# Scores of the next attention layer between the chunks of the MoE before it, on one Trainium2 core

## The reference, cut to what matters

```
h = layernorm(x) ; h = h @ ternary(w1).T + b1 ; h = gelu(h) ; h = layernorm(h) ; out = h @ ternary(w2).T + b2
```

## Time and profile before

| | us |
|---|---|
| median of 3 runs | 1383.3 (1379.87 to 1383.82) |
| the profiled execution | 1383.42 |
| its span, first to last instruction | 1381.6 |
| PE busy | 1198.1 (87%) |
| DVE busy | 927.3 (67%) |
| ACT busy | 697.0 (50%) |
| POOL busy | 269.1 (19%) |
| mean granted PE clock | 0.948 of full |

### The profile page before, as it was taken

One profiled execution on the slowest core, in us unless ns is written; L12 is line 12 of the kernel. 1 busy time (PEld: TensorE's weight loads), 2 busy tenths in 40 slices (PEclk: granted clock), 3 DMA queues, 4 the chain that ended last, 5 costly groups with the idle time before them and its releaser, 6 DMA issues.

```text
span 1381.6 us, 26337 instructions
## 1 busy us (share of the span) xinstructions
PE 1198.1 (87%) x7977; PEld 634.2 (46%) x8062; DVE 927.3 (67%) x2470; ACT 697.0 (50%) x1268; POOL 269.1 (19%) x560
## 2 busy tenths in 40 slices
PE   3436999999889998899999999999999979989876
PEld 1222223323356655445554555556666534445445
DVE  5867678687465555767778777755555476668676
ACT  2221676776644434556656666663222226666543
POOL 2332211211000012222332332110000211222112
PEclk7565999999999999999999999999999989999988
DMA  8312222310000003313333322100000202221001
GB/s 208 123 51 73 101 59 99 121 35 20 1 1 1 0 1 120 105 53 105 121 94 109 96 77 71 49 3 4 1 1 0 76 12 67 78 77 44 3 0 31
DMA packets 65199, 79.14 MB, mean 57 GB/s; under 512 B 5483, under 2 KB 58068, under 8 KB 64602
## 3 DMA queue, kind: packets, MB, share of 16 engines
q1 hardware_dynamic: 65098, 77.89, 18.0%
HBM read 45.27 MB, written 31.72 MB: 56 GB/s over the span
## 4 chain that ended last, share of the span: by engine, by line
PE 60%; issue 14%; DVE 8%; DMA 6%; ACT 5%; DVEq 3%; POOL 2%; SPq 1%; POOLq 1%; another core or an unknown queue 0%; ACTq 0%
PE bank L1633 11%; PE bank L1618 10%; PE bank L1602 9%; PE bank L1785 6%; PE bank L1786 6%; PE bank L1803 5%; PE bank L1586 3%; DMA KS<-scr_k 3%; PE bank L1620 2%; PE bank L1522 1%; ACT PT L921 1%; DVE M L1198 1%; PE bank L1582 1%; DVE N L1035 1%; PE bank L1516 1%
## 5 line engine op out<-in xcount | busy, mean ns | idle before, releaser
L921 ACT ACTIVATE PT<-bank 128x512 f32<-128x512 f32 (+1 forms) x784 | 425.3, 568 | 257.3 <-PE bank L1620 186.9
L1602 PE MATMUL bank<-KS,QS 125*128 125x512 bf16 (+3 forms) x1024 | 311.2, 332 | 37.1 <-DVE M L1195 13.6
L1198 DVE TENSOR_REDUCE M<-bank 128x1 f32<-128x512 f32 (+2 forms) x400 | 257.5, 684 | 89.3 <-PE bank L1602 53.1
L1195 DVE CUSTOM_DVE_ANT_0 masked_scores<-bank,maskw 128x384 bf16<-128x384 f32 (+1 forms) x384 | 228.6, 622 | 93.7 <-PE bank L1602 85.2
L1618 PE MATMUL bank<-QS,KS 128*128 128x256 bf16 (+1 forms) x953 | 277.4, 320 | 12.3 <-ACT PT L921 8.4
L1633 PE MATMUL bank<-PT,VA 128*32 128x512 f32 (+3 forms) x2048 | 211.6, 485 | 1.3 <-ACT PT L921 1.0
L1618 PEld LDWEIGHTS bank<-QS,KS 128*128 128x128 bf16 x1024 | 99.5, 98 | 222.5 <-ACT PT L921 158.9
L1620 PE MATMUL bank<-identb,maskw 128*128 128x128 bf16 x768 | 148.0, 219 | 12.3 <-issue 6.4
L1602 PEld LDWEIGHTS bank<-KS,QS 125*128 125x128 bf16 x1024 | 100.8, 99 | 115.2 <-DVE M L1198 30.3
L1785 PE MATMUL bank<-XT,MW 128*128 128x512 f32 (+1 forms) x232 | 120.5, 601 | 10.2 <-DVE PT L1375 5.9
L1803 PEld LDWEIGHTS bank<-MW,PT 128*128 128x128 f32 x864 | 110.8, 192 | 40.3 <-issue 37.7
(11 more groups left out here) (229 smaller groups left out, 1453.6 us busy)
## 6 DMA issues: line engine op xcount, KB each, us to landing
scr_q<-PQ SPq DMA_DIRECT2D x48, 384.0 KB, 3.2
QS<-scr_q SPq DMA_DIRECT2D x64, 288.0 KB
scr_k<-PK SPq DMA_DIRECT2D x24, 384.0 KB, 3.7
KS<-scr_k SPq DMA_DIRECT2D x32, 288.0 KB
QS<-MSB SPq DMA_DIRECT2D x192, 4.0 KB
MW<-in_m_w SPq DMA_DIRECT2D x3, 1024.0 KB, 8.2
MW<-in_m_w SPq DMA_DIRECT2D x3, 832.0 KB
scr_k<-PK SPq DMA_DIRECT2D x24, 96.0 KB, 1.9
```

Source lines behind the costliest of these rows:

```text
L921: a.activation(PT[kt % 2][:, js[0]:js[-1] + 1, q0:T], tiles(bank[st_bank(L, g, i)][:, 0:w * len(js)], len(js)), ACT.Exp, scale=c["scale"]) ...
L1195: v.tensor_tensor_reduce(masked_scores[S_ORDER[L][i]][:, 0:kl], bank[S_ORDER[L][i]][:, 0:kl], maskw[:, T - kl:T], -1.0, FLT_MAX, ALU.add, ...
L1198: v.tensor_reduce(M[g % 2][:, t * GH + js[0]:t * GH + js[-1] + 1], tiles(bank[S_ORDER[L][i]][:, 0:kl * len(js)], len(js)), AX_X, ALU.max, ...
L1602: r = mm(s, QS[0:ROWS_SHIFT, g * GH + j, t * P:(t + 1) * P], KS[0:ROWS_SHIFT, kv_slot(L, g, j), 0:kl], start=True, stop=not by_pe)
```

## The change

It has four parts.

1. The first pass of unit 0 of the chains that follow a MoE runs in the last MoE block, one item after the down matmuls of a chunk (`EARLY_S`: chunks 1 to 4 and 6 to 12), all into bank 7. DVE takes the maximum in the same chunk. POOL splits these maxima at the end of its last MoE block. The preparation of the next chain's block 0 moves from the last MoE block to the one before (`START_BLOCK`), and ACT's casts stand up to one chunk earlier.
2. At the start of those chains only items 0 to 4 of unit 1 run by themselves (`FIRST_S`), with the shift transposes of unit 0 after item 2. Items 5 to 10 of unit 1 and all of unit 2 run within unit 0: two of them after each of its first six items, one after each later one (`score_passes`). The shift of unit 1 stands at item 6 of unit 0. Sum and statistics of the last MoE block stand beside items 2 and 4 of unit 1 on DVE, its norm at item 6 of unit 0, its transposes and copy at items 8 and 9 of unit 1.
3. The loops over blocks 1 and 2 of attention layers and MoEs are written out, and with them the XTS copies go.
4. In the FFN the bias is split into three bf16 parts (by POOL, once, in the first block of L2's MoE) and added on PE by a second matmul into the same bank; `ffn_bias` goes, and GELU reads the bank.

```diff
+START_BLOCK = NB - 2
+EARLY_S = {1: 0, 2: 1, 3: 2, 4: 3, 6: 4, 7: 5, 8: 6, 9: 7, 10: 8, 11: 9, 12: 10}
+FIRST_S, FIRST_SHIFT_AT = 5, 2
+START_SUM_AT, START_STATS_AT = 2, 4
+START_NORM_AT, START_XT_AT, START_OUT_AT = (0, 6), (1, 8), (1, 9)
+def shift_at(L, b, g):
+    return 6 if L and is_first(b) and g == 0 and any(L == c[0] for c in CHAINS) else SHIFT_T_AT
+def score_passes(L, b, g, i):
+    ahead = neighbours(L, b, g)[2]
+    if L and is_first(b) and g == 0 and any(L == c[0] for c in CHAINS):
+        todo = [((L, 0, 1), k) for k in range(FIRST_S, NI[L])] + [(ahead, k) for k in range(NI[L])]
+        twice = len(todo) - NI[L]
+        return todo[2 * i:2 * i + 2] if i < twice else todo[twice + i:twice + i + 1]
+    return [(ahead, i)] if ahead and i < NI[ahead[0]] else []
-        def sequence(L, unit, Fori):
-            for g in range(NG):
-                unit(L, 0, g)
-            with Fori(1, NB - 1) as b:
+        def sequence(L, unit):
+            for b in range(NB):
                 for g in range(NG):
                     unit(L, b, g)
...
             def moe_pool(p):
-                for_inner_blocks(pool, body)
-                start_pool(AFTER[p])
-                post(p, NB - 1)
+                    if b == START_BLOCK:
+                        start_pool(AFTER[p])
+                    if is_last(b):
+                        shift(AFTER[p], 0, 0)
+                for b in range(NB):
+                    body(b)
...
                             v.scalar_tensor_tensor(U1[c % 2], bank[2 + c % 2][:, :], cc("m_b3", c), A1[c % 2], ALU.add, ALU.mult).then_inc(u_ready, 1)
+                            early(c)
                             dve.wait_ge(s1_ready, b * n + c + 1)
...
-            def score(L, b, g, i):
+            def score(L, b, g, i, early=False):
+                to = bank[7] if early else bank[S_ORDER[L][i]]
-                at_least(pe, max_done, item(L, b, g, i) + 1 - s_back(L, i))
+                at_least(pe, max_done, item(L, b, g, i) + 1 - (1 if early else s_back(L, i)))
+                if early:
+                    pe.wait_ge(xt_evac, NB * LAYERS[L]["phase"] - (2 if i < 4 else 1))
...
             def attention_pe(L):
-                    for g in range(2):
+                    for i in range(FIRST_S if L else 0):
+                        if L == 3 and i == S_ORDER[L].index(5):
+                            pe.wait_ge(summed, NB * E)
+                        score(L, 0, 1, i)
+                        if i == FIRST_SHIFT_AT:
+                            shift_t(L, 0, 0)
+                    for g in range(0 if L else 2):
...
             def moe_pe(p):
-                        if is_last(b) and c in PE_START[p]:
+                        if b == START_BLOCK and c in PE_START[p]:
                             prep_pe(AFTER[p], 0, PE_START[p][c])
+                        if is_last(b) and c in EARLY_S:
+                            score(AFTER[p], 0, 0, EARLY_S[c], True)
...
             def ffn_up(b):
-                    at_least(pe, fb_ready, (b - 1) * NT + i + 1)
-                    mm(bank[i][:, :], blk(XT, b)[:, i * P:(i + 1) * P], FW1[:, :], start=True, stop=True).then_inc(fu_ready, 1)
+                    at_least(pe, fg_ready, (b - 1) * NT + i + 1)
+                    mm(bank[i][:, :], blk(XT, b)[:, i * P:(i + 1) * P], FW1[:, :], start=True, stop=False)
+                    mm(bank[i][:, :], pick_parts[:, :], up_bias[:, :], start=False, stop=True).then_inc(fu_ready, 1)
```

More of the change, by code:

```diff
@@ L420, in item @@
             return (b * NG + g) * NI[L] + (ITEM_BASE[L] + i)
-        def sequence(L, unit, Fori):
-            for g in range(NG):
-                unit(L, 0, g)
-            with Fori(1, NB - 1) as b:
+        def sequence(L, unit):
+            for b in range(NB):
                 for g in range(NG):
                     unit(L, b, g)
-            for g in range(NG):
-                unit(L, NB - 1, g)
         def xt_bank(p, b):
@@ L732, in attention_pool @@
                 if starts_chain(L):
-                    shift(L, 0, 0)
+                    if L == 0:
+                        shift(L, 0, 0)
+                    else:
+                        post_root(p - 1, NB - 1)
                     shift(L, 0, 1)
@@ L752, in unit, with split_up_bias @@
                         shift(*ahead)
-                sequence(L, unit, pool.Fori)
+                sequence(L, unit)
+            def split_up_bias():
+                row = rc("f_b1")
+                g.memset(pick_parts[:, :], 0.0)
+                g.tensor_copy(up_bias[:, :], row)
+                pool.drain()
+                for i in range(PARTS):
+                    g.memset(pick_parts[32 * i:32 * i + 1, :], 1.0)
+                    pool.drain()
+                g.tensor_tensor(up_rest[:, :], row, up_bias[:, :], ALU.subtract)
+                pool.drain()
+                for i in (1, 2):
+                    g.tensor_copy(up_bias[32 * i:32 * (i + 1), :], up_rest[32 * i:32 * (i + 1), :])
+                    pool.drain()
+                g.tensor_tensor(up_rest[64:96, :], up_rest[64:96, :], up_bias[64:96, :], ALU.subtract)
+                pool.drain()
+                g.tensor_copy(up_bias[64:96, :], up_rest[64:96, :]).then_inc(bias_split, 1)
+                pool.drain()
             def moe_pool(p):
@@ L928, in unit @@
                             o_out(L, u - 1, g - 1)
-                        if follow and i == SHIFT_T_AT + 1:
+                        if follow and i == shift_at(L, b, g) + 1:
                             m_out(*follow)
+                        if L and starts_chain(L) and is_first(b) and (g, i) == START_OUT_AT:
+                            xt_out(p - 1, NB - 1)
                         if end and g == 0 and i == AO_OUT_AT:
@@ L1182, in prep_dve, with reduce @@
                                     ALU.mult).then_inc(prep_evac, 1)
-            def reduce(L, b, g, i):
+            def reduce(L, b, g, i, early=False):
                 t, js = S_ITEMS[L][i]
                 kl = k_to(L, t)
+                src = bank[7] if early else bank[S_ORDER[L][i]]
                 dve.wait_ge(s_ready, item(L, b, g, i) + 1)
@@ L1234, in unit @@
                     for i in range(NI[L]):
-                        if ahead and i < NI[ahead[0]]:
-                            reduce(*ahead, i)
+                        for unit_ahead, k in score_passes(L, b, g, i):
+                            reduce(*unit_ahead, k)
+                        if L and starts_chain(L) and is_first(b) and (g, i) == START_NORM_AT:
+                            post_norm(p - 1, NB - 1)
                         if prep:
@@ L1394, in body @@
                             gates_out(p, NB - 1, bank[7], c > LATE_T_AT)
-                        if is_last(b) and c in DVE_START[p]:
+                        if b == START_BLOCK and c in DVE_START[p]:
                             prep_dve(AFTER[p], 0, DVE_START[p][c])
-                for_inner_blocks(dve, body)
+                for b in range(NB):
+                    body(b)
                 if p == L2_MOE:
@@ L1452, in _ @@
             attention_dve(3)
-            def ffn_bias(b):
-                at_least(dve, ft_ready, (b - 1) * 4)
-                for i in range(NT):
-                    dve.wait_ge(fu_ready, b * NT + i + 1)
-                    v.tensor_tensor(HG[b % 2][:, i, :], bank[i][:, :], rc("f_b1"), ALU.add).then_inc(fb_ready, 1)
             def ffn_stats(b):
@@ L1574, in prep_pe @@
                         pe.wait_ge(xt_evac, post_index(L0_LINEAR, 0) + 1)
+                    if L and starts_chain(L) and b == 1:
+                        pe.wait_ge(y_added, NB * c["phase"])
                 w = attn_weights(L)[("q", "qs", "k", "ks", "v").index(what)]
@@ L1691, in unit @@
                         score_t(L, b, g, i)
-                        if ahead:
-                            score(*ahead, i)
+                        for unit_ahead, k in score_passes(L, b, g, i):
+                            score(*unit_ahead, k)
                         if prep:
@@ L1702, in unit @@
                                 values(L, b, g, kt)
-                        if follow and i == SHIFT_T_AT:
+                        if follow and i == shift_at(L, b, g):
+                            if (b, g) == (0, START_XT_AT[0] + 1) and L and starts_chain(L):
+                                pe.wait_ge(xt_evac, NB * p)
                             shift_t(*follow)
+                        if L and starts_chain(L) and is_first(b) and (g, i) == START_XT_AT:
+                            pe.wait_ge(m_evac, U(L, 0, g + 1) + 1)
+                            xt(p - 1, NB - 1, bank[7])
                         if prev and prev[2] % 2 and i == O_T_AT:
```

76 lines of the change are left out of this document (46 added, 30 removed).

## The result

The changed kernel takes 1359.3 us (median of 4 runs, 1356.7 to 1363.4) against 1381.6 in the same rounds (4 runs, 1379.2 to 1383.8): a ratio of 0.984, interval 0.981 to 0.987, so 21.8 us less by the ratio (17.5 to 26.2). The forecast was 17.0 less, 1366, with a range from 1359 to 1378: right in sign, and the time 0.3 us inside the range's edge. The profiled execution took 1359.4, its span 1357.5, the mean granted clock 0.957.

What follows compares the result with a forecast made beforehand. PE was taken to bound MoE and attention, with holes at two seams where DVE and DMA carry the path, and the FFN a PE, ACT, DVE chain. 6.3 + 6.7 + 3.0 + 1.0 = 17.0 off 1383.4 gives 1366 us, range 1359 to 1378.

Steps and rivals of the forecast that it cites:

- First seam: Hand-over from L1's MoE to the second chain: start 9.1 us earlier, less 1.8 and 1.0, so 6.3 gained.
- a sign of error: First units after the seams: forecast 16 and 18 us; the prediction counts as wrong if one exceeds 18.5.
- the store's: Second chain's first unit: the K store ends a longer unit, so the third unit's shift comes about 1.8 us later.
- the clock's: First units after both seams: half clock after PE's pause costs 1.0 and 1.5 us, bounds 0 and 2 each.
- Second seam: Hand-over from L2's MoE to the third chain: 10.5 us earlier, less 1.65, 0.45, 1.5 and 0.2, so 6.7 gained.
- the 0.2 in that sum: Second seam: a 0.2 us deduction in the net of 6.7, given without explanation.
- FFN bias: FFN: bias on PE ends PE's last-turn pause (2.5) and low clock (1.5), less 0.9; 3.0 us gained, bounds -0.9 and 9.9.
- Unrolling: Blocks 1 and 2 of attention and MoE: loops cost about nothing, eight ACT copies go; 1.0 us gained, bounds 0 and 4.8.
- D (code fetches): Written-out blocks: up to 17 more instruction packets, each stopping PE 1.7 us, 29 us; slower, 1395; chance 0.07.
- C (nothing is won): Seams: gain only moved, as block 1's stacks arrive late and a DMA wait takes it; about 1380; chance 0.05.
- A: First units grow 5 instead of about 3 us, MoE's chunks 5 instead of 2.7; about 1375; chance 0.20.
- B: Clock stays up (2.5), passes hide in PE's waits, FFN gains 5, copies 3; about 1357; chance 0.13.

Runs made afterwards that it cites:

- first seam only: Changed kernel, but the third attention starts as in the kernel before; ratio 0.9882 to the kernel before, median 1365.0 us.
- the run that kept it up: Changed kernel plus idle PE matmuls (12 and 10) in the waits before the two seams' first transposed scores; ratio 0.9851 to the kernel before, median 1360.8 us.
- the bias kernel: Kernel before with only the FFN's up bias added on PE instead of by DVE; ratio 0.9972 to the kernel before, 3.9 us less.

## Why the prediction was right, and where it was wrong

**First seam, 6.3 forecast, 6.2 measured** (first seam only, less loops and bias, uncertain by some 4 us); by stretches C to E, 3.6 (changed) and 5.3 (first seam only) against the loops written out. That the two totals agree to 0.1 us is luck, as the terms show. The shift came at 547.76, 10.9 us earlier, and the first transposed scores at 552.65, 10.4 earlier, where 9.1 was forecast (1.1 of the 10.4 was already won ahead of C, so 9.3 are the seam's): from MoE's last matmul 5.58 us against 5.1. The early passes cost 2.2 (C), not 2.7. The first unit took 18.7 us instead of 16: it passed the 18.5 that I had named as a sign of error. 2.25 of that is the low clock, by the run that kept it up; I had charged 1.0. Keeping the clock up won the kernel nothing in that run, for the reason that I had given for another term: what counts there is when the store comes. The K store came 5.0 us earlier than in the earlier trace rows (572.58 against 577.59), and the third unit 5.0 with it (583.01 against 588.01). The two terms act on one wait and should not have been added: the store's is the larger, 10.4 less 5.0 = 5.4 instead of 1.8, and the clock's is in it. The net is 9.3 less 5.4 = 3.9 in this profile, not 6.3: the start came as forecast, and the part given back was put at 2.8 where the rows show 5.4.

The Trainium skill, "TensorE: Matmul & The Clock Gate", Why this matters for your kernels, says that idle gaps bring back half rate. The trace agrees here: 0.50 behind both pauses, full clock behind the filled one. What it can't tell is whether anything waits for PE then.

**Second seam, 6.7 forecast, 5.5 measured** as what is left over, uncertain by some 5 us; 7.1 by stretches G to I against the loops written out. Scores 5.94 us behind the last matmul (5.8 forecast), first unit 16.2 (18 forecast). L2's MoE grew by 3.6 instead of the 2.7 of the passes; the 0.2 in that sum stands there without a reason. The clock was charged with 1.5, and the run that kept it up gained 1.0 there.

**FFN bias, 3.0 forecast, 3.9 measured.** The terms were put at the last turn, 2.5 for the pause and 1.5 for the clock, 4.0 in all; it gave 2.0, since the pause only fell to 1.33 (1.09 in the bias kernel). The most, 3.9, came around the first turn, whose wait the prediction does not mention: 5.46 and 1.75 became 3.52 and 0.43. The added matmuls took part of this back. So this total is near for the wrong reason.

**Unrolling, 1.0 forecast, 6.2 measured, outside its bounds (0 to 4.8).** This is the step that failed. I read 46.4 us for an interval "unrolled" and 45.8 for one "in the loop", and took them as equal. Both intervals contain looped units, and they are different stretches of work. The right comparison is the same interval in both forms. In the changed kernel:

```profile
763.02 1.16 PE L1582 MATMUL bank<-WC,AOT 128*128 128x128 f32 x8
...
808.97 1.16 PE L1582 MATMUL bank<-WC,AOT 128*128 128x128 f32 x8
...
853.97 1.16 PE L1582 MATMUL bank<-WC,AOT 128*128 128x128 f32 x8
```

45.95 and 45.00, so 0.4 and 0.8 less; all loops written out gives 46.03 and 44.98. The trace of before could not show the second form. It did show the sign that I passed over: PE's short waits for DVE's maxima and H, with "issue" ahead of DVE's instructions. Between 592 and 1096 us those waits make 2.7 of the 6.2; where the rest lies is open. The cap of 4.8 was eight copies of 0.6 us, a bound on the wrong thing: the copies did not show.

**The rivals.** D (code fetches) is refuted in its price. The instruction queue went from 51 packets and 0.84 MB to

```profile
q8 instruction: 65, 1.06, 0.3%
```

14 more where I had allowed 17, and writing the loops out gained. (Its 1.7 us for a small DMA is in no row; in the earlier trace rows and SP's queue 1.4 us pass from the end of the last shift DMA's issue, at 561.71, to the scores at 563.09.) The Trainium skill, "Runtime: NRT & Kernel Launch", Instruction fetch mechanics, has straight code prefetched, and a taken branch stalling when its target is outside what has been fetched. The sign agrees; but the one engine whose loop cost stands clear of none was DVE, and the gaps found in its rows lie inside the blocks, and some in blocks outside the loop. Whether they are fetches is not shown. C (nothing is won) did not happen, A only in the first unit of the first seam. B's time, 1357, was closer than mine, but not its reasons: the FFN gained 3.9, not 5, the copies did not show, and keeping the clock up gained nothing in the whole; what it lacked was the loops.

So the sum was 17.0 = 6.3 + 6.7 + 3.0 + 1.0, and the runs say 21.8 = 6.2 + 5.5 + 3.9 + 6.2: three terms within 1.2 us, which is closer than the runs can measure and closer than their inner terms came, and the fourth 5 us too small.

## What to carry to other kernels

Compare a looped with a written-out block only over the same work; where the trace has but one form, bound the loop by the waits that other engines have for it, not by what the loop adds on its own engine. When a unit starts earlier, follow the queue that feeds the units after it: a gain upstream of a DMA wait (the clock's 2.25 us here) is worth nothing until that wait is shortened. And in a queue that works strictly in order, put the transfers whose conditions have long been met ahead of the one that has to wait; moving the one load that was urgent behind it took the gain back.

## What was not expected of the hardware

The granted clock falls to half for some 4 us at places that differ from kernel to kernel. One is regular: near 412, in L1's first MoE block, in all nine profiles of kernels in which every engine's loops are written out, and in none of the five of kernels in which one or more are kept. The windows there, the kernel before, then the changed one:

```profile
410.00:412.00 2.00, 1.62 (x14) 1.19 (x12) 1.39 (x5) 0.35 (x1) 0.00 (x0) 1.00 0.00 0
412.00:414.00 2.00, 0.85 (x2) 0.49 (x3) 1.35 (x2) 1.16 (x3) 0.00 (x0) 1.00 0.01 4
```

```profile
410.00:412.00 2.00, 1.51 (x2) 0.70 (x3) 1.30 (x3) 0.83 (x2) 0.00 (x0) 0.66 0.00 0
412.00:414.00 2.00, 2.00 (x3) 0.59 (x3) 0.98 (x2) 0.00 (x0) 0.00 (x0) 0.50 0.00 0
```

Around this place PE has waits of 1.4 and 1.5 us for DVE both with loops (408.06 and 413.15 in the kernel before) and without (406.81 and 412.25 in the kernel with nothing but its loops written out), and of these two only the kernel before keeps the clock at full. Between the two waits the second kernel has a third, of 0.25 us; the kernel with DVE's loops alone written out has all three (405.92, 409.23, 411.37) and no fall. The fall costs 1.4 to 1.9 us (B is 80.5 to 81.0 in the kernels that have it alone, 79.1 before); the three profiles that also have a fall near 350 have a B of 81.5 to 82.3. Others came at 586, 606, 680, 1024 or 1078, among other places, each in one or a few of the profiles. Near 1024 a fall is worth about 1.7 us (in the changed kernel and its variants with early passes in L2's MoE, G is 201.8 without and 203.4 or 203.5 with it). They are part of the scatter of a few us between executions; how large a part is not shown. Why one pair of waits brings the clock down and the same pair elsewhere does not is open.
